# One core, four layers, one in-order queue per engine: the order of the stages written out anew

## What is computed

```python
# layer 0, the fusion
m = memory @ W_mem.T;  context = softmax(x @ m.T / 16) @ m
fused = x + sigmoid([x, context] @ W_gate.T + b_gate) * context ;  x = rmsnorm(fused)
# layer 1: two experts, "v" and "l"; vm, from the token types, picks one for each token
y = rmsnorm(x);  q, k, v = where(vm, y @ v_qkv, y @ l_qkv);  q, k = rotary(q), rotary(k)
ctx = softmax(causal(q @ k.T / 4)) @ v                       # 16 heads of 16
x = x + where(vm, ctx @ v_dense, ctx @ l_dense)
x = x + cross_attention(rmsnorm(x) @ cq_w, memory @ ckv_w) @ cdense_w   # 16 heads of 8
y = rmsnorm(x);  x = x + where(vm, silu(y @ v_gate) * (y @ v_up) @ v_down, same with l)   # 688 wide
# layer 2: 16 heads of 64 over the memory, then a gelu feed forward, 1024 wide
x = x + tanh(attn_gate) * softmax(masked(layernorm(x) @ Wq, memory @ Wkv)) @ Wo
x = x + tanh(ff_gate) * gelu(layernorm(x) @ W1) @ W2
# layer 3: as layer 1, with weights of its own
```

## Time and profile before

| what | value |
|---|---|
| device time, three runs | 1384.2, 1384.94, 1384.14 us |
| median | 1384.2 us |
| span of the profiled execution | 1380.9 us |
| time of the profiled execution beside its span | not given; the median is 3.3 us above the span |
| TensorE busy | 1306.9 us |
| VectorE busy | 764.5 us |
| ScalarE busy | 473.6 us |
| GpSimd busy | 452.1 us |

### The profile page before, as it was taken

The page is one execution under the profiler, slowest core; times in us unless marked ns, Lnnn a source line. Parts: engine busy times, 40 slices in busy tenths (PEclk is TensorE's granted clock), DMA queues, the critical chain, the costliest instruction groups (busy, mean ns, idle before and its releaser), DMA issues.

```text
span 1380.9 us, 25903 instructions
## 1 busy us (share of the span) xinstructions
PE 1306.9 (95%) x10931; PEld 1047.3 (76%) x10931; DVE 764.5 (55%) x1361; ACT 473.6 (34%) x785; POOL 452.1 (33%) x559
## 2 busy tenths in 40 slices
...
DMA packets 19901, 27.29 MB, mean 20 GB/s; under 512 B 3432, under 2 KB 15552, under 8 KB 19520
## 3 DMA queue, kind: packets, MB, share of 16 engines
...
## 4 chain that ended last, share of the span: by engine, by line
PE 84%; DVE 6%; ACT 5%; POOL 3%; issue 2%; ACTq 0%; DVEq 0%; POOLq 0%
PE bank L1433 6%; PE bank L1723 6%; PE bank L1688 5%; PE bank L1693 5%; PE bank L1577 5%; PE bank L1933 4%; PE bank L1940 4%; PE bank L1897 4%; PE row_banks L1527 4%; PE row_banks L1837 3%; PE row_banks L1560 3%; PE bank L1495 3%; PE bank L1712 3%; PE bank L1426 3%; PE row_banks L1532 2%; ACT room L2051 2%
## 5 line engine op out<-in xcount | busy, mean ns | idle before, releaser
L1283 POOL TENSOR_SCALAR_AFFINE_SELECT room<-room 128x1024 f32<-128x1024 f32 x64 | 70.7, 1107 | 185.3 <-ACT room L2051 185.3
L2293 DVE TENSOR_REDUCE room<-row_banks 128x4 f32<-128x512 f32 (+1 forms) x128 | 116.4, 952 | 23.1 <-PE row_banks L1532 22.8
L2051 ACT ACTIVATE room<-row_banks 128x1536 f32<-128x1536 f32 x64 | 92.9, 1451 | 90.0 <-PE row_banks L1560 90.0
L1723 PE MATMUL bank<-room,down_w 128*128 128x256 f32 x384 | 95.9, 391 | 0.5 <-DVE room L2393 0.5
L2307 DVE RECIPROCAL room<-bank 128x256 f32<-128x256 f32 x32 | 56.1, 1754 | 59.3 <-PE bank L1577 59.3
L2083 ACT ACTIVATE room<-bank 128x256 f32<-128x256 f32 x96 | 36.4, 383 | 148.6 <-PE bank L1693 137.6
L1245 POOL TENSOR_TENSOR room<-room 128x256 f32<-128x256 f32 x32 | 24.5, 767 | 173.0 <-ACT room L2063 173.0
L1723 PEld LDWEIGHTS bank<-room,down_w 128*128 128x128 f32 x384 | 70.4, 192 | 14.0 <-issue 4.9
L1357 POOL TENSOR_TENSOR room<-room 128x512 f32<-128x512 f32 x32 | 33.7, 1070 | 133.1 <-DVE room L2495 132.9
L1560 PE MATMUL row_banks<-room 32*128 32x256 f32 (+1 forms) x1024 | 62.1, 357 | 9.7 <-ACT room L2051 4.6
L1560 PEld LDWEIGHTS row_banks<-room 32*128 32x128 f32 x1024 | 48.9, 190 | 27.6 <-issue 15.6
...
## 6 DMA issues: line engine op xcount, KB each, us to landing
...
```

The costliest lines, as they stand in the source:

```text
L1283: pool.affine_select(out=diagonal, in_=diagonal, compare_op=ALU.is_ge, fill=0.0, base=0, pattern=[[0, 8], [1, P]], channel_multiplier=-1)\
L1723: return pe.matmul(ff_bank[0][:, t * S:(t + 1) * S], down_w[:, f, t * P:(t + 1) * P], hid[:, i, :], start=(i == t == 0), stop=(i == UPS - ...
L2051: act.activation(probs[w % 2], row_banks[:, :, 0:3 * P], ACT.Exp).then_inc(*ATT_ACT.does(e, f"exp{w}"))
L2293: last = dve.tensor_reduce(dst, row_banks[:, :, P * i:P + S * i], X, ALU.max, negate=True)
```

## The change

It takes out the tables of offsets and starting times and writes the order of each engine as one list of words, stage.example.number. Each engine has its list; whole_order() only reads them. The stages are the same ones, with the same instructions, buffers and waits: 1150 on TensorE, 613 on ScalarE, 723 on VectorE, 401 on GpSimd and 8 on SyncE. Against the order before, 894 pairs of stages are the other way round on TensorE (592 of its positions hold another stage), 454 on ScalarE (376), 463 on VectorE (407), 303 on GpSimd (247), none on SyncE.

```diff
@@ -167,823 +167,346 @@
-def fuse_stages():
...
-    put(-9564.6366, "f_add")
-    put(-9564.2232, "f_rstd")
-    put(-780.2099, "f_shift")
-    put(-779.9075, "f_sums")
-    put(-772.2775, "f_gated")
...
-LOAD_STARTS = [-612.096, -499.670, -490.195, -380.642, -369.655, -285.215, -252.600, -251.912]
...
+ORDER = {
+    "pe": """
+        x_turn.0 x_turn.1 x_turn.2 x_turn.3 x_turn.4 x_turn.5 f_scores.0 f_scores.1 x_turn.7 x_turn.6 p_vec.0
+        f_scores.2 p_trig.0 f_scores.3 f_turn.1 f_mem.0.0 f_mem.0.1 f_turn.2 f_turn.0 f_mem.0.2 f_context.1
+        f_context.2 f_context.0 f_gate.2 f_gate.1 f_turn.3 f_context.3 f_sum.2 f_gate.0 f_spread.2 f_gate.3 f_sum.1
+        f_mem.0.3 f_sum.0 f_spread.1 f_spread.0 f_sum.3 f_scores.4 f_scores.5 f_scores.6 f_spread.3 f_turn.4 n0_sum.0
+        f_scores.7 f_turn.5 f_context.4 f_context.5 n0_spread.0 f_gate.4 f_turn.7 f_turn.6 f_gate.5 f_context.6
+        f_context.7 f_sum.4 f_gate.6 f_gate.7 q.0 k.0 f_sum.5 f_spread.4 f_sum.6 f_sum.7 f_spread.5 v.0 f_spread.6
+        f_spread.7 n0_sum.1 n0_spread.1 first_scores.0.0 q.1 first_scores.0.1 k.1 first_scores.0.2 v.1
+        first_scores.0.3 n0_sum.2 n0_spread.2 turn_max.0 second_scores.0.0 second_scores.0.1 values.0.0
+        second_scores.0.2 values.0.1 second_scores.0.3 first_scores.1.0 values.0.2 values.0.3 first_scores.1.1 q.2
...
+        values.7.0 second_scores.7.2 values.7.1 second_scores.7.3 late_up.5.1 cross_second.6 late_up.5.2 values.7.2
+        cross_values.6 values.7.3 down.5.0 cross_project.6 down.5.1 late_down.5.0 down.5.2 crs_sum.6.1 down.5.3
+        late_down.5.1 crs_spread.6.1 late_down.5.2 down.5.4 memory.7 down.5.5 dense.7 up.6.0 a_center.0 crs_sum.7.0
+        up.6.1 crs_spread.7.0 up.6.2 cross_q.7 a_sum.0 cross_first.7 a_spread.0 up.6.3 up.6.4 cross_turn_max.7
+        a_keys.0.0 cross_second.7 up.6.5 a_keys.0.1 a_q.0.0 cross_values.7 a_vals.0.0 a_q.0.1 a_q.0.2 a_q.0.3
+        a_scores.0.0 a_scores.0.1 a_vals.0.1 down.6.0 cross_project.7 a_scores.0.2 down.6.1 down.6.2 down.6.3
+        a_scores.0.3 crs_sum.7.1 a_turn.0.0 down.6.4 a_turn.0.1 crs_spread.7.1 down.6.5 a_values.0.1 a_values.0.0
...
+        a_vals.1.1 b_down.0.1 b_down.0.2 b_up.0.3 a_scores.1.3 b_down.0.3 a_turn.1.0 a_turn.1.1 b_down.0.4
...
+        first_scores.9.3 crs_spread.8.0 cross_q.8 cross_first.8 turn_max.9 q.11 second_scores.9.0 k.11
+        second_scores.9.1 values.9.0 cross_turn_max.8 second_scores.9.2 values.9.1 second_scores.9.3 cross_second.8
...
+        cross_second.15 up.14.5 cross_values.15 down.14.0 cross_project.15 down.14.1 down.14.2 crs_sum.15.1 down.14.3
+        crs_spread.15.1 down.14.4 down.14.5 up.15.0 up.15.1 up.15.2 up.15.3 up.15.4 up.15.5 late_up.15.0 late_up.15.1
...
+    """,
+    "dve": """
+        f_shift.0 p_one_hot.0 f_shift.1 f_shift.2 f_sums.1 p_trig_out.0 f_sums.0 f_sums.2 f_shift.3 f_gated.2 f_sums.3
+        f_gated.1 f_mean.2 p_seen.0 f_gated.0 f_mean.1 f_gated.3 f_mean.0 f_y.1 f_y.0 f_mean.3 f_y.2 f_shift.4
+        f_sums.4 f_shift.5 f_y.3 f_sums.5 n0_mean.0 f_shift.6 f_shift.7 f_sums.6 f_sums.7 f_gated.4 n0_split.0
+        f_gated.5 f_mean.4 n0_y.0 f_gated.6 f_gated.7 flip_q.0 f_mean.5 f_mean.7 flip_k.0 f_y.4 f_mean.6 f_y.5 add_k.0
...
+        late_hidden.5.0 late_hidden.5.1 late_hidden.5.2 cross_context.6 crossed.6 context.7.1 crs_mean.6.1 post_y.6
+        cross_v_out.7 give.5 late_give.5 attended.7 hidden.6.0 crs_mean.7.0 a_centered.0 cross_y.7 hidden.6.1 a_mean.0
...
 def whole_order():
 
-    order = [(time, stage, 0, *which) for time, stage, *which in once_stages()]
-
-    def each(starts, stages, first=0):
...
-    def by_parity(starts, stages_of, layer):
-        for e in range(B):
-            order.extend((starts[layer][e] + time, stage, layer * B + e, *which) for time, stage, *which in stages_of(layer, e % 2))
...
-    return [(stage, e, *which) for _time, stage, e, *which in sorted(order)]
+    order = []
+    for stages in ORDER.values():
+        for word in stages.split():
+            stage, *at = word.split(".")
+            order.append((stage, *map(int, at)))
+    return order
```

More of the change, by code:

```diff
@@ L169 @@
 }
[L170 to L179, removed]
-def fuse_stages():
-    at = []
-    def put(time, stage, *which):
-        at.append((time, stage, *which))
-    put(-9564.6366, "f_add")
-    put(-9564.2232, "f_rstd")
-    put(-780.2099, "f_shift")
-    put(-779.9075, "f_sums")
-    put(-772.2775, "f_gated")
[L194 to L207, removed]
@@ L210, in norm_stages @@
[L210 to L253, removed]
@@ L256, in project_stages @@
[L256 to L316, removed]
-        put(-795.5664, "v_out")
-        put(-773.2386, "k_mask")
-        put(-760.2458, "q_mask")
-        put(678.2822, "q")
-        put(679.6758, "k")
-        put(681.0539, "v")
-    return at
@@ L902, in final_stages @@
-def final_stages():
-    at = []
-    def put(time, stage, *which):
-        at.append((time, stage, *which))
-    put(-9564.6367, "out_sent")
-    put(-24.1953, "out")
-    put(1485.6441, "turn_out")
-    return at
-def once_stages():
-    at = []
-    def put(time, stage, *which):
-        at.append((time, stage, *which))
-    put(-9125.4755, "p_vec_out")
-    put(-9009.7270, "f_mem_out", 0)
-    put(2269.6313, "p_one_hot")
-    put(2270.2195, "p_trig_out")
-    put(2272.2799, "p_seen")
-    put(2455.0669, "a_zero")
-    put(2634.1904, "f_mem_out", 1)
-    put(2641.9461, "f_mem_out", 2)
-    put(2642.8294, "f_mem_out", 3)
-    put(4467.6526, "p_vec")
-    put(4508.4445, "f_mem", 0)
-    put(4596.4685, "p_trig")
-    put(4597.0345, "f_mem", 1)
-    put(4604.8206, "f_mem", 2)
-    put(4605.0045, "f_mem", 3)
-    return at
```

871 lines of the change are left out of this document (297 added, 574 removed).

## The result

The changed kernel takes 1377.36 us in the median of four runs (1375.08 to 1379.41), against 1384.32 for the kernel before: a ratio of 0.9947, with a 95% interval of 0.9933 to 0.9962. That is 7.0 us faster where I had said 15. The profiled execution took 1375.08 us with a span of 1372.8, so 8.1 us less span than before. The profiled execution is the fastest of the four; the four differ by 4.3 us, which is itself something to explain.

What follows compares the result with a forecast made beforehand. TensorE, busy 1306.9 of 1380.9 us, was taken as the bound, with idle time at four seams. Terms -5.4 (fusion with ramp), -6.0, -1.2, -1.3, -1 sum to -14.9: 1384.2 to 1369 us; own range 1361 to 1377, overall 1359 to 1384.

Steps and rivals of the forecast that it cites:

- (a): The fusion, 36-75 us: moved stages and waits make f_gate.7 end 3.7 us later, bounds 0 and +7.
- My 1.5 us for p_seen.0: In the fusion: p_seen.0, now behind f_gated.1 on VectorE, delays f_gated.0, so TensorE's f_sum.0 and f_sum.1 wait: +1.5 us.
- (b): The ramp, f_gate.7's end to q.1's first matmul: 19.75 us against 28.85, so -9.1, bounds -12 and -5.
- The 2.9 us: In the ramp: time left ahead of q.0, where eight loads of flags into registers stand in its queue.
- the ramp gives back what it gains: Rival, chance 0.18: gates end later, q.0 starts at half clock and GpSimd queues, +10 us in all, 1379 us.
- Two signs: Prediction wrong if f_gate.7 ends after 82 us, or TensorE's granted clock in 105-180 us falls below 0.89.
- (c): The join of layer 1 into layer 2, 500-605 us: reordered stages fill TensorE's waits, -6.0 us, bounds -7.3 and -2.
- (d): Layer 2 into layer 3, 895-1010 us: one wait filled, another opened, -1.2 us, bounds -3 and +2.
- (e): The end: down.14 stages fill waits around cross_project.15 and crs_sum.15.1, about -1.3 us, bounds -2 and 0.
- (f): Everything else (180-500, 605-895, 1010-1300 us), with 9.2 us idle: -1 us, bounds -4 and +6.
- The slower case: Rival, chance 0.11: in layer 2 seven examples each get a new TensorE wait of 3.2 us, +22.4, 1392 us.
- one rule: VectorE instructions with two SBUF operands and GpSimd ones reading SBUF block each other; some 1 us later at q.1.

## Why the prediction was right or wrong

- **What bounds the kernel** was right: TensorE, at four seams; its busy time stayed (1306.9 and 1306.5), and all that moved was waits and clock.
- **(a), the fusion, is the step that failed.** "+3.7, bounds 0 and +7" measured +12.4 at f_gate.7's end. Three things in it:
  - The waits up to f_scores.4 are +6.9, at the edge of the bound. My 1.5 us for p_seen.0 were right in size (1.4 to 2.2) and wrong in the way: they came through GpSimd, whose f_rstd.2 stood still beside VectorE's two-input operation, and not through f_gated.0. Missing altogether was f_tanh.3 ahead of f_square.0 on ScalarE, 1.8 us. I had read VectorE's list against TensorE's, and not ScalarE's. With both taken away 3.8 us remain for the other moves, where I had 1.3 and 0.9. By the means of the traces some 2.4 of them lie ahead of the first gate, which begins at 28.4 to 29.2 us in the old order and at 30.2 to 32.0 in the new; I had put 0.43 us on an f_context, which takes 1.0.
  - The half clock over full work, 5.5 us, had no term in my sum at all. I had named the clock for q.0 and k.0, as a bound of (b), and looked at it where the old kernel had it. With the old fusion put back it doesn't come there (1.00 from 36 to 74 us), so the new order of the fusion brings it; what in that order does is open.
- **(b), the ramp, was right in the main**: -9.1 forecast, -9.9 measured; the gain is there. That the sum is so near is partly luck, for two of its terms were off and nearly cancel. The 2.9 us "that q.0's weight load waits for nothing the profile shows" measured nothing: q.0 begins at 87.26, with f_gate.7's end. That wait needs no loads into registers to explain it. The row of q.0 itself names VectorE's line 2249 as what it waited for the earlier trace rows, and that operation of n0_y.0 ended at 87.20, just before q.0's 87.38:

```profile
86.51 0.69 DVE L2249 TENSOR_TENSOR room<-room 128x512 f32<-128x512 f32 x1
```

  In the new order n0_y.0 is done long before. No run shows that the loads cost anything. Against this, v.0 got the half clock, for which the sum had no term: it takes 4.44 us against 2.81. The rival "the ramp gives back what it gains" (0.18, 1379) is nearest to the time that came, and a later end of the gates is part of its mechanism; but it had 3.3 us for that where 8.7 were missing, and its half clock on q.0 didn't come, so that its number is near is luck too.
- **Behind the ramp** I took the clock of 105-180 to be unchanged. It fell to 0.84, and q.3 came 2.1 us later: from q.1 to q.3 TensorE is busy 67.59 us where it was 64.80, and idle 13.91 where it was 14.61. With the old fusion and the new ramp it is the same (67.76 and 13.91), and with the old start it is not (64.85), so the new ramp gives back 2.1 of its 9.9 us there. Two signs that I had named for a wrong prediction came, this one and f_gate.7's end behind 82.
- **(c), the join, was right** in mechanism and low in size: -6.0 forecast, -7.9 in the table. dense.7 waits 0.55 us where it waited 1.69, and of the waits at a_keys, a_turn and a_values none is left in this list:

```profile
PE bank L956 <- DVE room L1845: 0.5, 1, 0.5
PE bank L970 <- POOL room L850: 0.5, 1, 0.5
```

- **(d), (e), (f)** gave -4.4 for -3.5. At the end cross_project.15 waits 1.28 us instead of 2.34:

```profile
1335.98 1.13 PE L1187 MATMUL bank<-room,cd_w 128*128 128x256 f32 x4 [1.28 <-DVE room L1881]
```

- **The slower case** was not it: layer 2 gained 2.3 us, with no wait in each example. The 4.1 us idle in its stretch are four waits, of which the longest, 2.25 us, is in the old order as well, at 898.84.
- **The range** is too narrow upwards for its own bounds. They lie 3.3, 4.1, 4.0, 3.2, 1.3 and 7.0 us above the terms of (a) to (f), and the root of their squares is 10, not 8; the -11 and -1 for (a) with (b) come out of neither a sum nor a root of theirs. The time came 0.4 us above the range.

The clock may also be behind the spread. The kernel before has 34 runs between 1381.91 and 1385.08 us and one of 1392.14; the mean clock is 0.980 or 0.981 in all of the former that have one on record, and 0.974 in the latter. The changed kernel's four runs spread over 4.3 us, and most of the kernels with new order in the fusion or the ramp over 3 to 7 us. The same kernel with the old start took 1369.36 us at 0.984 and 1376.61 at 0.980, as if a stretch at half clock came in one run and not in the next. But this isn't shown, since one run of each kernel has a trace, and the one with f_square.0 and p_seen.0 moved took 1373.26 us at 0.979 and 1373.57 at 0.976.

I weighed one rule at q.1, where it would have cost 1 us. There n0_split.1 and n0_y.1 ran with GpSimd idle (103.84 to 106.26); what met was add_q.0 of VectorE (101.82 to 102.50) and n0_rstd.1 of GpSimd, which took 1.08 us instead of 0.70:

```profile
101.98 1.08 POOL L773 TENSOR_TENSOR room<-room,neg_half 128x2 f32<-128x2 f32 x1 [0.94 <-DVE room L1756]
```

The trace shows it far larger at another place: GpSimd's operation of 0.70 us took 3.02 beside VectorE's of 2.65, and 0.70 again once VectorE's was elsewhere. This is what the Trainium skill, "SBUF — State Buffer", section "Who interferes with whom", says of an instruction of VectorE with two inputs in SBUF and one of GpSimd that reads SBUF: the other blocks for the whole instruction. The trace agrees: the short one waits for the long one's end, however short it is.
